# The first microseconds of a graph layer: first pieces shared between two DMA queues, four parts for piece 0, 17 warm-ups, and a_lo in halves to piece 19

## The chip, the cores and the metric

The kernel runs on one core of a Trainium2 chip. A core has TensorE (matrix multiply), VectorE and ScalarE (elementwise work), GpSimd, SyncE (which here only issues transfers), and 16 DMA engines that move data between HBM and the on-chip memory SBUF. Engines run on their own and wait for each other through semaphores. The metric is the time of one execution on the device in microseconds, the median of several runs.

## The reference: what is computed

```python
def _layernorm(x, axis=-1, eps=1e-05):
    m = jnp.mean(x, axis=axis, keepdims=True)
    v = jnp.var(x, axis=axis, keepdims=True)
    return (x - m) / jnp.sqrt(v + eps)

def reference(x, adj, L0_gnn_h):          # x: 8192x128, adj: 8192x8192, L0_gnn_h: 8192x128, float32
    h = jnp.maximum(_layernorm(x, axis=-1), 0.0)
    return x + 0.9 * (adj @ h) + 0.1 * L0_gnn_h
```

(Condensed to its core.) The work is the product of a 256 MB matrix with a small one. Each element of `adj` is read once and used for one 128-wide row of h.

## The kernel before

The contraction runs over 64 blocks of 128 rows of x (`BLOCKS`). The output has 16 chunks of 512 rows (`CHUNKS`), each one PSUM bank wide. `adj` comes in 256 pieces of 1 MB, each 128 x 2048 floats: 128 rows of the contraction for four chunks, or four times 128 rows for one chunk. The first 128 pieces are "wide": for each block k, piece 2k covers chunks 0 to 3 and piece 2k+1 chunks 4 to 7, so all eight banks are filled side by side. The other 128 are "tall": 16 pieces in a row complete one of chunks 8 to 15. The host stores pieces 0 to 23 as two halves (`early_dram`), so that each half is a transfer of its own; the others are one transfer each.

The product is made in three passes of a faster 32-bit format, fp32r. ScalarE rounds a piece to `a_hi` (L284), VectorE makes the rest `a_lo` = raw - a_hi (L328), and h is split likewise into `h_hi` and `h_lo`. TensorE does, per piece, four matmuls a_hi x h_hi (L416), four a_hi x h_lo (L422) and four a_lo x h_hi (L427); for tall pieces the lines are L438, L439 and L443. Only pieces 0 and 1 (`NATIVE`) go unsplit, as plain fp32 matmuls of raw and `h_full` (L405), which need nothing but the transfer and block 0 of h; each such matmul appears in the trace as two passes.

The order on each engine is written by hand:

- SyncE (the `sync` block) issues x of block 0, then pieces in order. `raw` has 6 slots; pieces 6 and 7 wait until TensorE has used pieces 0 and 1, later ones until VectorE has made a_lo of the piece six before. x of later units of four blocks goes ahead of a certain piece by the table `LOAD_X_AT`, for unit 2 (blocks 8 to 11) ahead of piece 5.
- ScalarE issues x of blocks 1 to 3 and 4 to 7 (L273, L274), scales blocks 1 to 3 (L251), rounds them (L258), then rounds the pieces; `SCALE_AT` and `HIGH_H_AT` say behind which piece later units are scaled and rounded.
- VectorE makes statistics (L294, L304, L307) and normalises block 0 on its own (L355, L359), does units 0 and 1, makes `h_lo` of unit 0 (L320), then a_lo of the pieces. `STATS_AT`, `AGGREGATE_AT`, `SHIFT_AT` and `LOW_H_AT` say behind which piece the steps of later units come. GpSimd makes 1/sqrt(var) between `aggregate` and `make_shift`, and VectorE waits for it in `make_shift`.
- TensorE runs 15 matmuls on zeros (`WARM_UP`, L399), then the pieces. `a_hi` and `a_lo` have 3 slots.

`EARLY` = 24 pieces are loaded and rounded in halves, `EARLY_LOW` = 10: pieces 2 to 9 have a_lo made in halves, each with its own count of the semaphore that TensorE waits for.

## Time and profile before

| | us |
|---|---|
| median of 3 runs | 711.0 |
| lowest and highest | 710.96 and 711.1 |
| the profiled execution | 711.17 |
| its span, first to last instruction | 709.4 |
| TensorE busy in it | 703.6 (99%) |
| VectorE busy | 627.1 (88%) |
| ScalarE busy | 524.4 (74%) |
| DMA, mean over the span | 403 GB/s |

The span is shorter than the execution by 1.8 us of start and end. Times below are from the start of the span. In the trace PE is a matmul on TensorE, PEld its weight load (which overlaps), DVE is VectorE, ACT ScalarE, POOL GpSimd, and SPq and ACTq are the instructions by which SyncE and ScalarE issue a transfer. What stands in brackets behind a row is the idle time of the engine before it and what ended it. The end of a matmul is modelled, so spacings of starts are to be read, not durations.

### The profile page before, as it was taken

Reading aid. Unit: us, or ns where it says so; the run is one execution under the profiler, and the core shown is the slowest. Engines: PE = TensorE matmul, PEld = TensorE weight load, DVE = VectorE, ACT = ScalarE, POOL = GpSimd, SP = SyncE. Lnnn points to the kernel's source line nnn. Section 1 sums busy time; section 2 is a strip of 40 time slices with the busy share of each in tenths; the row PEclk is TensorE's granted clock in tenths of the full one; section 3 lists DMA queues with packets and bytes.
Section 4 is the critical chain, followed back from the end, with each engine's and each line's share of the span. In section 5 each row is a group of like instructions: output and inputs, shape, how many; then the busy total and the mean of one; then the engine's idle time right before and its main releaser. Section 6 shows DMA issues by size and latency. Waiting matters only on the chain.

```text
span 709.4 us, 7934 instructions
## 1 busy us (share of the span) xinstructions
PE 703.6 (99%) x3079; PEld 577.5 (81%) x3079; DVE 627.1 (88%) x474; ACT 524.4 (74%) x356; POOL 39.7 (6%) x23
## 2 busy tenths in 40 slices
PE   8999999999999999999999999999999999999998
PEld 4878888888888888888888888888888888888886
DVE  5889999999999989999898888888988898889885
ACT  5888787888777878788767677776767676767673
POOL 1001111011010111010000000000000000000000
PEclk9999999999999999999999999999999999999999
DMA  9999999999999999999999999999999999999990
GB/s 353 409 408 412 421 419 417 423 417 418 421 419 420 421 419 420 419 419 422 414 401 413 394 396 396 404 385 405 419 421 421 421 420 423 420 420 422 404 418 18
DMA packets 47557, 285.73 MB, mean 403 GB/s; under 512 B 5280, under 2 KB 5792, under 8 KB 17824
## 3 DMA queue, kind: packets, MB, share of 16 engines
q1 hardware_dynamic: 47232, 284.77, 98.2%
q8 instruction: 24, 0.39, 0.2%
q10 hardware_dynamic: 288, 0.46, 0.2%
q14 instruction: 13, 0.11, 0.0%
HBM read 281.02 MB, written 4.19 MB: 402 GB/s over the span
## 4 chain that ended last, share of the span: by engine, by line
PE 94%; DMA 3%; DVE 1%; SPq 1%; ACT 1%; issue 0%; DVEq 0%
PE acc L443 16%; PE acc L438 16%; PE acc L439 16%; PE acc L427 15%; PE acc L422 15%; PE acc L416 15%; DMA raw<-early_dram 3%; DVE a_lo L328 1%; SPq L206 1%; ACT a_hi L284 0%; ACT h_full L251 0%; DVE finished L347 0%; SPq L191 0%; DVEq L119 0%; DVEq L346 0%
## 5 line engine op out<-in xcount | busy, mean ns | idle before, releaser
L328 DVE TENSOR_TENSOR a_lo<-raw,a_hi 128x2048 fp32r<-128x2048 f32 (+1 forms) x262 | 581.4, 2225 | 59.4 <-ACT a_hi L284 58.6
L284 ACT ACTIVATE a_hi<-raw 128x2048 fp32r<-128x2048 f32 (+1 forms) x276 | 491.4, 1782 | 169.4 <-PE acc L443 100.1
L438 PE MATMUL acc<-a_hi,h_hi 128*128 128x512 f32 x512 | 199.2, 389 | 0.0
L439 PE MATMUL acc<-a_hi,h_lo 128*128 128x512 f32 x512 | 199.2, 389 | 0.0
L443 PE MATMUL acc<-a_lo,h_hi 128*128 128x512 f32 x512 | 136.8, 389 | 0.0
L427 PE MATMUL acc<-a_lo,h_hi 128*128 128x512 f32 x504 | 135.1, 390 | 0.2 <-DVE a_lo L328 0.2
L416 PE MATMUL acc<-a_hi,h_hi 128*128 128x512 f32 x504 | 135.2, 390 | 0.0
L422 PE MATMUL acc<-a_hi,h_lo 128*128 128x512 f32 x504 | 134.7, 389 | 0.0
L438 PEld LDWEIGHTS acc<-a_hi,h_hi 128*128 128x128 f32 x512 | 96.1, 188 | 20.0
L443 PEld LDWEIGHTS acc<-a_lo,h_hi 128*128 128x128 f32 x512 | 96.1, 188 | 20.0
L439 PEld LDWEIGHTS acc<-a_hi,h_lo 128*128 128x128 f32 x512 | 96.1, 188 | 19.9
L427 PEld LDWEIGHTS acc<-a_lo,h_hi 128*128 128x128 f32 x504 | 94.4, 188 | 20.6 <-DVE a_lo L328 1.1
L416 PEld LDWEIGHTS acc<-a_hi,h_hi 128*128 128x128 f32 x504 | 94.6, 188 | 20.2 <-issue 0.5
L422 PEld LDWEIGHTS acc<-a_hi,h_lo 128*128 128x128 f32 x504 | 94.6, 188 | 19.7
L244 POOL TENSOR_TENSOR rstd<-var_eps,exponent 128x4 f32<-128x4 f32 (+2 forms) x17 | 39.2, 2304 | 279.4 <-DVE var_eps L307 279.4
L251 ACT ACTIVATE h_full<-x_sb,shift,rstd 128x128 f32<-128x128 f32 x63 | 27.1, 479 | 4.5 <-DVE shift L313 4.5
L294 DVE BATCH_NORM_STATS2 stats<-x_sb 128x6 f32<-128x128 f32 x64 | 17.9, 286 | 3.3 <-DMA x_sb<-x_dram 3.3
L347 DVE SCALAR_TENSOR_TENSOR finished<-acc,residual 128x512 f32<-128x512 f32 (+1 forms) x17 | 11.0, 652 | 3.9 <-PE acc L443 3.9
L313 DVE SCALAR_TENSOR_TENSOR shift<-mean_var,rstd 128x4 f32<-128x4 f32 (+1 forms) x16 | 2.6, 161 | 12.0 <-POOL rstd L244 12.0
L336 DVE SCALAR_TENSOR_TENSOR residual<-res_sb 128x512 f32<-128x512 f32 x16 | 10.9, 683 | 0.0
L320 DVE TENSOR_TENSOR h_lo<-h_full,h_hi 128x512 fp32r<-128x512 f32 x16 | 10.8, 676 | 0.0
L258 ACT ACTIVATE h_hi<-h_full 128x512 fp32r<-128x512 f32 x16 | 9.8, 614 | 0.1
(15 smaller groups left out, 29.4 us busy)
## 6 DMA issues: line engine op xcount, KB each, us to landing
raw<-tall_dram SPq DMA_DIRECT2D x128, 1024.0 KB, 8.0
raw<-wide_dram SPq DMA_DIRECT2D x104, 1024.0 KB, 11.1
raw<-early_dram SPq DMA_DIRECT2D x48, 512.0 KB, 11.7
res_sb<-res_dram SPq DMA_DIRECT2D x16, 512.0 KB, 9.8
out_dram<-finished SPq DMA_DIRECT2D x15, 256.0 KB, 8.2
x_sb<-x_dram SPq DMA_DIRECT2D x14, 256.0 KB, 11.5
x_sb<-x_dram ACTq DMA_DIRECT2D x1, 256.0 KB, 4.6
out_dram<-finished SPq DMA_DIRECT2D x2, 128.0 KB, 1.8
```

The costliest lines, as they stand in the source:

```text
L244: nc.gpsimd.tensor_tensor(rstd[:, a:b], var_eps[:, a:b], exponent[:, 0:b - a], ALU.pow).then_inc(rstd_ready, 1)
L251: last = nc.scalar.activation(h_full[:, in_h(k), :], x_sb[:, in_x(k), :], ACT.Relu, bias=shift[:, k:k + 1], scale=rstd[:, k:k + 1])
L284: nc.scalar.activation(a_hi[:, q % SPLIT_SLOTS, cols], raw[:, q % RAW_SLOTS, cols], ACT.Copy).then_inc(hi_ready, 1)
L294: return nc.vector.bn_stats(stats[:, k, :], x_sb[:, in_x(k), :])
L328: nc.vector.tensor_tensor(a_lo[:, q % SPLIT_SLOTS, cols], raw[:, q % RAW_SLOTS, cols], a_hi[:, q % SPLIT_SLOTS, cols].bitcast(fp32), ALU.s ...
L347: nc.vector.scalar_tensor_tensor(out=finished[:, n % 2, cols], in0=acc[:, c % WIDE, cols], scalar=1.0 - ALPHA, in1=residual[:, n % RES_RIN ...
L416: nc.tensor.matmul(acc[:, quad * QUAD + j, :], h_hi[:, k, :], a_hi[:, slot, cols], start=False, stop=False)
L422: nc.tensor.matmul(acc[:, quad * QUAD + j, :], h_lo[:, k, :], a_hi[:, slot, cols], start=False, stop=False)
L427: last = nc.tensor.matmul(acc[:, quad * QUAD + j, :], h_hi[:, k, :], a_lo[:, slot, cols], start=False, stop=(k == BLOCKS - 1))
L438: nc.tensor.matmul(bank, h_hi[:, k, :], a_hi[:, slot, cols], start=(k == 0), stop=False)
L439: nc.tensor.matmul(bank, h_lo[:, k, :], a_hi[:, slot, cols], start=False, stop=False)
L443: last = nc.tensor.matmul(bank, h_hi[:, k, :], a_lo[:, slot, cols], start=False, stop=(k == BLOCKS - 1))
```

## The change

- `EARLY_LOW` goes from 10 to 20: a_lo of pieces 10 to 19 is made in halves too.
- Piece 0 is loaded in four parts of 512 columns. Parts 1 and 3 of it and the second half of piece 1 (`BY_SCALAR`) are issued by ScalarE, the others by SyncE. x of block 0 is loaded in two halves of 64 partitions, one by each. ScalarE issues x of blocks 4 to 7 last.
- x of blocks 8 to 11 goes ahead of piece 7 instead of 5, and its statistics, aggregates and shift move with it; its scaling stays.
- VectorE makes h_lo of unit 0 ahead of the statistics of blocks 4 to 7, and the shift of unit 1 behind a_lo of piece 2.
- In the wide pieces TensorE does hi and lo on the first two segments, then hi and lo on the last two, then a_lo on all four.
- 17 warm-ups for 15.

```diff
-EARLY, EARLY_LOW = 24, 10
+EARLY, EARLY_LOW = 24, 20
 PARTS = {_q: 2 for _q in range(EARLY)}
+PARTS[0] = 4
...
+BY_SCALAR = [(0, 1), (0, 3), (1, 1)]
...
-LOAD_X_AT = {}
-STATS_AT, AGGREGATE_AT, SHIFT_AT = {}, {}, {}
...
+LOAD_X_AT = {7: 2}
+STATS_AT, AGGREGATE_AT, SHIFT_AT = {7: [8, 9], 8: [10, 11]}, {8: 3}, {NATIVE: 2, 10: 3}
...
-WARM_UP = 15
+WARM_UP = 17
...
+        def load_part(engine, q, i, cols):
+            n = PARTS[q]
+            at = (i % (n // 2)) * (PIECE // n)
+            engine.dma_start(raw[:, q % RAW_SLOTS, cols],
+                             adj_early[q, i // (n // 2), :, at:at + PIECE // n]
+                             ).then_inc(part_landed[q % RAW_SLOTS][i], 16)
...
+                if q in PARTS:
+                    for i, cols in parts(q):
+                        if (q, i) not in BY_SCALAR:
+                            load_part(sp, q, i, cols)
...
-            load_x(0, 0, 1)
+            sp.dma_start(x_sb[0:P // 2, 0, :], x[0:P // 2, 0, :]).then_inc(x_landed[0], 16)
...
+            act.dma_start(x_sb[P // 2:P, 0, :], x[P // 2:P, 0, :]).then_inc(x_landed[0], 16)
             act.dma_start(x_sb[:, 1:UNIT, :], x[:, 1:UNIT, :]).then_inc(x_landed[1], 16)
+            for q, i in BY_SCALAR:
+                load_part(act, q, i, dict(parts(q))[i])
             act.dma_start(x_sb[:, UNIT:2 * UNIT, :], x[:, UNIT:2 * UNIT, :]).then_inc(x_landed[2], 16)
...
+            low_h(0)
             for k in range(UNIT, 2 * UNIT):
                 wait_x(k)
                 last = statistics(k)
             last.then_inc(stats_ready, 1)
             aggregate(2)
-            make_shift(2)
-            low_h(0)
...
-                for j in range(QUAD):
...
+                for half in (range(0, QUAD // 2), range(QUAD // 2, QUAD)):
+                    for j in half:
...
+                        nc.tensor.matmul(acc[:, quad * QUAD + j, :], h_hi[:, k, :], a_hi[:, slot, cols],
+                                         start=False, stop=False)
...
+                    for j in half:
+                        cols = slice(j * SEG, (j + 1) * SEG)
+                        nc.tensor.matmul(acc[:, quad * QUAD + j, :], h_lo[:, k, :], a_hi[:, slot, cols],
+                                         start=False, stop=False)
```

VectorE at its start, before: from the statistics of blocks 1 to 3 to the a_lo of pieces 2 to 5 (`128x1024` is a half piece).

```order
L294 BN_STATS stats<-x_sb 128x6 x3
L304 BN_AGGR mean_var<-stats 128x2 x3
L307 TENSOR_SCALAR var_eps<-mean_var 128x3
L313 SCALAR_TENSOR_TENSOR shift<-mean_var,rstd 128x3
L294 BN_STATS stats<-x_sb 128x6 x4
L304 BN_AGGR mean_var<-stats 128x2 x4
L307 TENSOR_SCALAR var_eps<-mean_var 128x4
L313 SCALAR_TENSOR_TENSOR shift<-mean_var,rstd 128x4
L320 TENSOR_TENSOR h_lo<-h_full,h_hi 128x512
L328 TENSOR_TENSOR a_lo<-raw,a_hi 128x1024 x8
```

The same place in the changed kernel (its line numbers are 12 or 13 higher).

```order
L306 BN_STATS stats<-x_sb 128x6 x3
L316 BN_AGGR mean_var<-stats 128x2 x3
L319 TENSOR_SCALAR var_eps<-mean_var 128x3
L325 SCALAR_TENSOR_TENSOR shift<-mean_var,rstd 128x3
L332 TENSOR_TENSOR h_lo<-h_full,h_hi 128x512
L306 BN_STATS stats<-x_sb 128x6 x4
L316 BN_AGGR mean_var<-stats 128x2 x4
L319 TENSOR_SCALAR var_eps<-mean_var 128x4
L340 TENSOR_TENSOR a_lo<-raw,a_hi 128x1024 x2
L325 SCALAR_TENSOR_TENSOR shift<-mean_var,rstd 128x4
L340 TENSOR_TENSOR a_lo<-raw,a_hi 128x1024 x8
```

h_lo stands ahead of the second group of statistics, and the second shift has a_lo of piece 2 ahead of it.

ScalarE's start, before: two transfers of x, then its own work.

```order
L273 DMA x_sb<-x_dram 128x384
L274 DMA x_sb<-x_dram 128x512
L251 ACT_TABLE_LOAD
L251 ACTIVATE h_full<-x_sb,shift,rstd 128x128 x3
L258 ACTIVATE h_hi<-h_full 128x512
L284 ACTIVATE a_hi<-raw 128x1024 x4
```

And in the changed kernel.

```order
L282 DMA x_sb<-x_dram 64x128
L283 DMA x_sb<-x_dram 128x384
L184 DMA raw<-early_dram 128x512 x2
L184 DMA raw<-early_dram 128x1024
L286 DMA x_sb<-x_dram 128x512
L259 ACT_TABLE_LOAD
L259 ACTIVATE h_full<-x_sb,shift,rstd 128x128 x3
```

x of blocks 4 to 7 (`128x512`) is now the sixth transfer of this queue instead of the second.

## Rows read from the trace of the kernel before

**Rows 1.** The page, part 4: the chain that ended last, by engine.
```profile
PE 94%; DMA 3%; DVE 1%; SPq 1%; ACT 1%; issue 0%; DVEq 0%
```
**Rows 2.** Windows: stretch, us, busy us (count) of PE, PEld, DVE, ACT, POOL; PEclk; DMA.
```profile
100.00:200.00 100.00, 100.00 (x443) 82.81 (x442) 93.32 (x89) 80.89 (x62) 13.36 (x5) 1.00 1.02 420
600.00:700.00 100.00, 100.00 (x443) 82.81 (x442) 87.44 (x43) 71.00 (x37) 0.00 (x0) 1.00 0.93 383
```
**Rows 3.** Timeline of the start: start us, us, engine, line, operation, count.
```profile
1.10 3.38 PE L399 MATMUL acc<-warm 128*128 128x256 bf16 x15 [1.10 <-POOL warm L239]
...
4.79 0.29 DVE L359 TENSOR_SCALAR h_full<-x_sb,rstd 128x128 f32<-128x128 f32 x1 [0.63 <-POOL rstd L244]
...
5.71 8.66 PE L405 MATMUL acc<-raw,h_full 128*128 128x512 f32 x16 [1.23 <-DMA raw<-early_dram]
...
7.55 0.34 PEld L405 LDWEIGHTS acc<-raw,h_full 128*128 128x128 f32 x1 [0.52 <-issue]
...
8.40 0.34 PEld L405 LDWEIGHTS acc<-raw,h_full 128*128 128x128 f32 x1 [0.52 <-issue]
...
9.05 5.31 PE L405 MATMUL acc<-raw,h_full 128*128 128x512 f32 x12
```
**Rows 4.** Timeline of TensorE at pieces 3, 10 and 20.
```profile
16.98 1.07 PE L416 MATMUL acc<-a_hi,h_hi 128*128 128x512 f32 x4
...
38.17 1.20 PE L427 MATMUL acc<-a_lo,h_hi 128*128 128x512 f32 x4 [0.18 <-DVE a_lo L328]
...
64.03 1.08 PE L416 MATMUL acc<-a_hi,h_hi 128*128 128x512 f32 x4
```
**Rows 5.** Timeline of ScalarE: rounding the last half of piece 8 and piece 9.
```profile
28.17 1.06 ACT L284 ACTIVATE a_hi<-raw 128x1024 fp32r<-128x1024 f32 x1 [0.22 <-DMA raw<-early_dram]
30.89 1.06 ACT L284 ACTIVATE a_hi<-raw 128x1024 fp32r<-128x1024 f32 x1 [1.66 <-DMA raw<-early_dram]
32.17 1.06 ACT L284 ACTIVATE a_hi<-raw 128x1024 fp32r<-128x1024 f32 x1 [0.22 <-DMA raw<-early_dram]
```
**Rows 6.** DMA from 26.5 to 29 us: queue, packets, MB, share of 16 engines.
```profile
q8 instruction: 1, 0.02, 2.7%
```
**Rows 7.** Timeline: a_lo of piece 10, then pieces 25 to 27.
```profile
35.82 2.29 DVE L328 TENSOR_TENSOR a_lo<-raw,a_hi 128x2048 fp32r<-128x2048 f32 x1 [0.84 <-ACT a_hi L284]
...
74.28 1.92 ACT L284 ACTIVATE a_hi<-raw 128x2048 fp32r<-128x2048 f32 x1 [0.56 <-DMA raw<-wide_dram]
...
76.23 2.29 DVE L328 TENSOR_TENSOR a_lo<-raw,a_hi 128x2048 fp32r<-128x2048 f32 x1
...
82.20 2.29 DVE L328 TENSOR_TENSOR a_lo<-raw,a_hi 128x2048 fp32r<-128x2048 f32 x1
...
84.90 1.07 PE L427 MATMUL acc<-a_lo,h_hi 128*128 128x512 f32 x4
```
**Rows 8.** DMA issues before 1.5 us: count, KB, us from issue to landing.
```profile
raw<-early_dram SPq DMA_DIRECT2D x1, 512.0 KB, 4.4
x_sb<-x_dram ACTq DMA_DIRECT2D x1, 256.0 KB, 4.6
...
x_sb<-x_dram SPq DMA_DIRECT2D x1, 64.0 KB, 2.5
```
**Rows 9.** Timeline of VectorE: statistics of blocks 4 to 7, first a_lo.
```profile
7.28 0.87 DVE L294 BATCH_NORM_STATS2 stats<-x_sb 128x6 f32<-128x128 f32 x4
...
8.59 0.17 DVE L307 TENSOR_SCALAR var_eps<-mean_var 128x4 f32<-128x4 f32 x1
...
11.94 1.23 DVE L328 TENSOR_TENSOR a_lo<-raw,a_hi 128x1024 fp32r<-128x1024 f32 x1 [1.29 <-ACT a_hi L284]
```
**Rows 10.** Windows, as rows 2: the last two numbers are DMA share and GB/s.
```profile
4.00:4.50 0.50, 0.48 (x3) 0.00 (x0) 0.16 (x1) 0.00 (x0) 0.38 (x1) 1.00 0.97 356
...
5.00:5.50 0.50, 0.00 (x0) 0.00 (x0) 0.50 (x4) 0.00 (x0) 0.00 (x0) 1.00 1.04 410
5.50:8.00 2.50, 2.29 (x3) 1.18 (x4) 1.46 (x10) 0.60 (x2) 0.86 (x1) 1.00 1.03 419
```

34 lines of the change are left out of this document (11 added, 23 removed).

## The prediction, made before the changed kernel ran

> **What bounds the kernel now.** I read the chain of waits first, then the windows, the start of the timeline, the places where TensorE stalls, and last the transfers.
>
> The chain is TensorE for 94% of the span and DMA for 3% [rows 1]. Once it runs, TensorE is always busy: 443 matmuls in 100 us, in the wide half as in the tall half [rows 2]. From the hi-pass of piece 28 to the last matmul the spacing is 0.2267 us, and 12 × 0.2267 = 2.72 us make a piece. The change takes no matmul away, so all it can win is time in which TensorE was slow, idle or waiting. There are two such places.
>
> The start: warm-ups run to 4.48 us, the first real matmul starts at 5.71 with 1.23 us idle ahead of it, ended by a transfer; h_full was there at 4.79 + 0.29 = 5.08. Weight loads of the fp32 passes then start 0.85 us apart (7.55, 8.40); the twelve passes seen from 9.05 on start (5.31 − 0.59) / 11 = 0.43 apart [rows 3] (0.59 is one pass's own shown length). That is half speed and full speed, 1.2 and 2.4 GHz, though the granted clock reads 1.00 from 5.5 us on [rows 10].
>
> Early stalls: from the hi-pass of piece 3 (16.98) to that of piece 20 (64.03) it takes 47.05 us [rows 4], where 17 pieces need 17 × 2.72 = 46.24. So 0.81 us are lost, most of it ahead of piece 10's L427 at 38.17, where TensorE waits for a_lo [rows 4].
>
> What makes these stalls is the supply. A half piece lands every 1.28 us (30.89 and 32.17, where ScalarE starts on it), so a piece takes 2.56 us against TensorE's 2.72: the lead grows by 0.16 us a piece. And one landing came 1.44 us late (28.17 to 30.89 instead of 1.28) [rows 5]. In that stretch a single packet of queue 8, an instruction load, took 2.7% of 16 engines over 2.5 us, 1.07 us of one DMA engine [rows 6]. A half piece is spread over all engines and counts as landed with the last, so that one engine holds back every later landing.
>
> **The bound that the change doesn't touch.** After piece 20 TensorE never stalls, but its margins are thin, and the thinnest counts. It is piece 27's. ScalarE starts on piece 25 when it lands, at 74.28; VectorE makes a_lo of 25 from 76.23, then aggregates, a_lo of 26, a shift that waits for GpSimd, and a_lo of 27 from 82.20 to 84.49. TensorE begins on it at 84.90 [rows 7]. Where TensorE did stall, it started 0.06 us after a_lo: 35.82 + 2.29 = 38.11 [rows 7], then 38.17 [rows 4]. So the margin is 84.90 − 84.49 − 0.05 = 0.36 us. Pieces 24 to 27 keep whole loads and whole a_lo in the change, in the same VectorE order; their chain hangs on landings. **TensorE can arrive at piece 27 at most 0.36 us earlier; whatever more is won ahead of it becomes a wait there.**
>
> **Part by part.**
> x of block 0 in halves on two queues: whole, it took 2.5 us to land [rows 8]. Halved: 0 to 0.4 us earlier; I take 0.3, so h_full at 4.8.
> Piece 0 in four parts: its first half lands 4.4 us after issue now, together with x of 4 to 7 after 4.6 [rows 8], though that is 512 KB in 4 KB rows and this 256 KB in 2 KB rows: the two queues are served row by row. A first part of half the size, with x of 1 to 3 beside it alone, should land at 4.1 to 4.6, ahead of h_full.
> 17 warm-ups: fifteen filled 3.38 us [rows 3], two more at about 0.21 end near 4.9, where h_full comes. TensorE starts 0.8 us earlier, without a gap. The clock rises somewhere between the warm-ups' end and 8.7 as now: worth 0 to 1.6 us (three spacings of 0.85 and one of 0.66 against 0.43).
> Part (0,3) and half (1,1) wait their turn in their queues, to near 7.6 and 10.2, each about when TensorE wants them: 0 to 0.3 us lost. The fp32 pieces then end near 12 to 13 instead of 14.2.
> x of 4 to 7 is now the sixth transfer of ScalarE's queue and lands near 11 to 12 instead of 5.75. VectorE stands at it with its statistics, aggregates and var_eps, 7.28 to 8.76 now, 1.5 us [rows 9]; queued behind is a_lo of piece 2, which starts at 11.94 now [rows 9]. It will start at 12.3 to 13.6, and its two halves, 1.23 each with 1.14 between starts, end at 14.7 to 16.0; TensorE finishes the piece 0.45 later. So piece 3 starts at 16.0 to 16.8 (bounded below by the end of the fp32 pieces), say 16.4, against 16.98 now. Of some 2 us won at the start 0.6 is left here. ScalarE's scaling of blocks 4 to 7 waits some 0.4 us for the shift that stands behind this; the hi-pass has over 2 us of margin in pieces 4 to 6, which covers it.
> h_lo of unit 0 ahead of these statistics costs nothing; behind them it would have waited for x. The pass order hi, lo, hi, lo: the same matmuls, each with its own weight load before too; it wants the second half of a_hi 0.45 us later. A bank is revisited after two matmuls instead of four; tall pieces use one bank for all and run at 443 in 100 us too [rows 2].
> a_lo in halves to piece 19: two of 1.23 [rows 9] with overlapping starts, 2.37 us for 2.29 a piece, on an engine with idle time there. The first half comes 1.1 us earlier, and the last is wanted 0.45 later. The stalls up to piece 19 go: 0.81 us.
> x of 8 to 11 two pieces later: the halves of 5 and 6 land 0.64 us earlier, from 7 on nothing moves; its statistics move with it.
> The stream: same bytes, same engines, always some 10 us of transfers queued, so landings from piece 7 on move only if its rate does. While two queues were active it made 356 and later 410 GB/s, alone 419 [rows 10]. If two queues cost as in the first of these over 8 us, all lands 1.0 us later; if the start fills better, 0.3 earlier. I take 0.1 later, near the second.
> The Trainium skill ("Trainium Kernel Development and Optimization", Key Constraints) says that transfers of SP's and ACT's queues run on the same 16 engines, and that issuing from several only saves issue time. It speaks against any gain in the stream: by it the shift is 0 and the time 710.6.
>
> **The sum.** At piece 20 TensorE would be 0.6 + 0.81 = 1.4 us ahead; piece 27 lets 0.36 through; less 0.1 for the stream: 0.26. The profiled execution took 711.17 us with a span of 709.4; it would take 710.9 with 709.1. Against the median of 711.0: 710.7.
>
> **Rivals.**
> A, the forecast: capped at piece 27. With the stream's bounds of −0.3 and +1.0 the time is 710.3 to 711.6. Chance 0.70.
> B: the cap lifts. If the engine that was late at 30.89 isn't late before piece 25 (its load falls elsewhere), landings come up to 1.44 us earlier and the 1.4 us reach the end: 709.6, with a good start 709.4. For it: the load's time hangs on how far TensorE is in its program, which moves. Against: some engine always gets it. Chance 0.10.
> C, slower: two instruction loads fall on the same DMA engine. One did 1.44 us of harm, the later ones none that adds to it. If the next, near 58 us, adds, landings from piece 21 on come 1.44 later: 711.0 − 0.36 + 1.44 = 712.1, with 0.4 for two queues 712.5. It is a loss as soon as a_hi of piece 25 starts later than 74.28 + 0.36. Chance 0.10.
> D: x of 4 to 7 comes so late that VectorE holds TensorE up for good, or TensorE starts no earlier. Harmless until piece 3 starts after 16.98 + 0.81 − 0.36 = 17.4; beyond, each us costs one: 711.0 to 711.4. Chance 0.10.
>
> **How the numbers follow.** 0.2% is 1.4 us, about what a measurement can tell: below 709.6 is faster, above 712.4 slower. A and D lie within. Most of B is below (0.08), over half of C above (0.06); within: 0.86. A and D span 710.3 to 711.6; I widen to 709.9 and 711.7, which takes in what is near in B and C.
>
> **What would show it.** First real matmul near 4.9 without a gap behind the warm-ups; piece 3 between 16.0 and 16.8; no wait at pieces 10 to 19; new waits of TensorE for a_lo at pieces 20 to 27, some 1 us in all, the last at 27 with its a_lo ending near 84.5; a_hi of piece 25 starting within 0.3 us of 74.28. It would be wrong if piece 27's a_lo pass began more than 0.6 us ahead of 84.90, or if landings moved.

## The result and the profile after

| | before | after |
|---|---|---|
| median of 12 runs, us | 711.06 | 712.61 |
| lowest and highest | 710.96 and 712.06 | 712.25 and 713.21 |
| the profiled execution | 711.17 | 712.3 |
| its span | 709.4 | 710.5 |

The changed kernel is slower by 0.2%: after to before is 1.002, with a 95% interval of 1.0013 to 1.0028. The forecast of 710.7 and its range, to 711.7, missed. The spans of the two profiled executions, worked out to hundredths, are 709.35 and 710.47, so 1.12 us are to be explained. The medians lie 1.55 apart: the profiled execution of the changed kernel is one of its shorter ones, and the last experiment shows what a longer one looks like. Of all executions reported here four took 1018 to 4088 us; they move no median by more than 0.02 us, and of the two that were profiled (1845 and 1018 us) only the start is read.

The chain of waits of the changed kernel, by engine:

```profile
PE 97%; DMA 1%; DVE 1%; ACTq 0%; issue 0%; DVEq 0%
```

Read alone, this is better than the chain in [rows 1]: TensorE has 97% of it instead of 94. A share does not say how late TensorE was when it began to be busy. That stands in the timeline of the start (start us, us, engine, line, operation, count, idle before and what ended it):

```profile
0.74 0.57 SPq L225 DMA_DIRECT2D x_sb<-x_dram  x1
0.75 0.57 ACTq L282 DMA_DIRECT2D x_sb<-x_dram  x1
...
1.35 0.85 ACTq L283 DMA_DIRECT2D x_sb<-x_dram  x1
...
3.75 0.29 DVE L306 BATCH_NORM_STATS2 stats<-x_sb 128x6 f32<-128x128 f32 x1 [3.75 <-DMA x_sb<-x_dram]
...
5.28 0.29 DVE L372 TENSOR_SCALAR h_full<-x_sb,rstd 128x128 f32<-128x128 f32 x1 [0.63 <-POOL rstd L252]
```

x of block 0 is there at 3.73, not 0.3 us earlier than its 3.24 before but 0.5 later, and h_full starts at 5.28 against 4.79 in [rows 3]. The first real matmul gains almost nothing: 5.62 against 5.71. Then the timeline of TensorE to piece 3:

```profile
5.62 2.07 PE L417 MATMUL acc<-raw,h_full 128*128 128x512 f32 x2 [0.71 <-DVE h_full L372]
8.05 6.89 PE L417 MATMUL acc<-raw,h_full 128*128 128x512 f32 x14 [0.36 <-DMA raw<-early_dram]
14.38 1.02 PE L430 MATMUL acc<-a_hi,h_hi 128*128 128x512 f32 x2
...
17.20 0.73 PE L441 MATMUL acc<-a_lo,h_hi 128*128 128x512 f32 x2 [0.42 <-DVE a_lo L340]
18.34 0.73 PE L441 MATMUL acc<-a_lo,h_hi 128*128 128x512 f32 x2 [0.40 <-DVE a_lo L340]
18.91 0.63 PE L430 MATMUL acc<-a_hi,h_hi 128*128 128x512 f32 x2
```

TensorE waits for the second part of piece 0 until 8.05, and in piece 2 twice for a_lo. Four spacings of that piece are too long by 0.585, 0.114, 0.567 and 0.110, 1.38 us in all. Piece 3 starts at 18.91 instead of 16.98 in [rows 4]: 1.93 us late, of which 0.58 are there when piece 2 starts (14.38 against 13.80 before). VectorE shows why, at the place of [rows 9]:

```profile
14.54 0.87 DVE L306 BATCH_NORM_STATS2 stats<-x_sb 128x6 f32<-128x128 f32 x4 [3.51 <-DMA x_sb<-x_dram]
15.44 0.38 DVE L316 BATCH_NORM_AGGREGATE mean_var<-stats 128x2 f32<-128x6 f32 x4
15.85 0.17 DVE L319 TENSOR_SCALAR var_eps<-mean_var 128x4 f32<-128x4 f32 x1
15.93 2.35 DVE L340 TENSOR_TENSOR a_lo<-raw,a_hi 128x1024 fp32r<-128x1024 f32 x2
```

It stood for 3.51 us at x of blocks 4 to 7, which landed at 14.51 (5.75 before), with a_lo of piece 2 queued behind. After piece 3 TensorE never waits for an operand again; the 0.81 us lost between pieces 3 and 20 before (the waits at 10, 13 and 19) are gone. 1.93 − 0.81 = 1.12 us is the whole difference of the spans.

A second limit lies just beside it. ScalarE, VectorE and TensorE at pieces 25 to 27, as in [rows 7]:

```profile
75.62 1.92 ACT L296 ACTIVATE a_hi<-raw 128x2048 fp32r<-128x2048 f32 x1 [0.56 <-DMA raw<-wide_dram]
...
83.46 0.16 DVE L325 SCALAR_TENSOR_TENSOR shift<-mean_var,rstd 128x4 f32<-128x4 f32 x1 [0.90 <-POOL rstd L252]
83.54 4.49 DVE L340 TENSOR_TENSOR a_lo<-raw,a_hi 128x2048 fp32r<-128x2048 f32 x2
...
86.03 1.08 PE L441 MATMUL acc<-a_lo,h_hi 128*128 128x512 f32 x4
```

Piece 25 comes at 75.62 instead of 74.28: the stream of pieces is 1.34 us late there. a_lo of piece 27 starts at 83.54, takes 2.29 and ends at 85.83, 0.20 before TensorE wants it, so the margin is 0.15. Had TensorE not been late by itself, this would have made the kernel −0.36 + 1.34 = 0.98 us slower.

Where the stream lost its time stands in the windows, as [rows 10] (the last two numbers are DMA share and GB/s). The changed kernel:

```profile
3.50:4.00 0.50, 0.50 (x4) 0.36 (x3) 0.24 (x1) 0.00 (x0) 0.00 (x0) 1.00 0.80 166
4.00:4.50 0.50, 0.50 (x5) 0.29 (x2) 0.43 (x4) 0.00 (x0) 0.00 (x0) 1.00 0.87 219
4.50:5.00 0.50, 0.41 (x2) 0.00 (x0) 0.15 (x1) 0.39 (x1) 0.40 (x1) 1.00 0.91 229
5.00:5.50 0.50, 0.00 (x0) 0.00 (x0) 0.22 (x1) 0.50 (x1) 0.16 (x1) 1.00 0.93 264
6.00:7.00 1.00, 1.00 (x2) 0.12 (x1) 0.93 (x7) 0.00 (x0) 0.00 (x0) 1.00 1.07 424
...
2.00:9.00 7.00, 5.93 (x17) 2.69 (x16) 2.43 (x13) 1.97 (x3) 1.42 (x2) 1.00 0.91 302
```

and the kernel before, over the last of these stretches:

```profile
2.00:9.00 7.00, 5.77 (x16) 2.96 (x15) 3.68 (x22) 2.45 (x5) 1.58 (x3) 1.00 1.00 378
```

From 4 to 5.5 us the change moved 219 to 264 GB/s where [rows 10] has 356 to 410. From 6 us on both run at full rate, with two queues active too (424). Over 2 to 9 us it is 302 against 378, (378 − 302) × 7 us = 0.53 MB, which at 410 GB/s is 1.3 us. The loss is made before 6 us.

The trace holds sixteen completions for each transfer, one of each DMA engine, and the transfer counts as landed with the last. For the second half of piece 7 the mean of the sixteen is 1.41 us later than before and the last one 1.59; for piece 25 it is 1.40 and 1.34. So the mean loss stays as it was made. What changes on the way is the last engine, and the table of the stream below comes back to it.

### The profile page after: what moved, and what is told of

It reads as the page before. It is cut to its first block, busy times and chain, and to the rows that moved or that the text cites. A ratio compares the mean times of both kernels' runs of the same rounds, so it can differ in the third digit from the quotient of the medians.

```text
span 710.5 us, 7951 instructions
## 1 busy us (share of the span) xinstructions
PE 704.3 (99%) x3081; PEld 577.6 (81%) x3081; DVE 626.6 (88%) x484; ACT 523.6 (74%) x356; POOL 40.4 (6%) x23
## 3 DMA queue, kind: packets, MB, share of 16 engines
q10 hardware_dynamic: 800, 1.54, 0.6%
## 4 chain that ended last, share of the span: by engine, by line
PE 97%; DMA 1%; DVE 1%; ACTq 0%; issue 0%; DVEq 0%
PE acc L457 16%; PE acc L453 16%; PE acc L452 16%; PE acc L441 16%; PE acc L436 16%; PE acc L430 16%; DMA x_sb<-x_dram 1%; DVE a_lo L340 0%; ACTq L184 0%; DVE stats L306 0%; ACTq L283 0%; ACTq L282 0%; DVE finished L359 0%; DVE mean_var L316 0%; DVEq L122 0%
## 5 line engine op out<-in xcount | busy, mean ns | idle before, releaser
L452 PE MATMUL acc<-a_hi,h_hi 128*128 128x512 f32 x512 | 199.2, 389 | 0.0
L453 PE MATMUL acc<-a_hi,h_lo 128*128 128x512 f32 x512 | 199.2, 389 | 0.0
L430 PE MATMUL acc<-a_hi,h_hi 128*128 128x512 f32 x504 | 155.5, 390 | 0.0
L436 PE MATMUL acc<-a_hi,h_lo 128*128 128x512 f32 x504 | 155.2, 389 | 0.0
L306 DVE BATCH_NORM_STATS2 stats<-x_sb 128x6 f32<-128x128 f32 x64 | 17.7, 286 | 7.6 <-DMA x_sb<-x_dram 7.6
L417 PE MATMUL acc<-raw,h_full 128*128 128x512 f32 x16 | 9.0, 708 | 1.1 <-DVE h_full L372 0.7
## 6 DMA issues: line engine op xcount, KB each, us to landing
raw<-wide_dram SPq DMA_DIRECT2D x104, 1024.0 KB, 11.2
```

Source lines behind the costliest of these rows:

```text
L306: return nc.vector.bn_stats(stats[:, k, :], x_sb[:, in_x(k), :])
L430: nc.tensor.matmul(acc[:, quad * QUAD + j, :], h_hi[:, k, :], a_hi[:, slot, cols], start=False, stop=False)
L436: nc.tensor.matmul(acc[:, quad * QUAD + j, :], h_lo[:, k, :], a_hi[:, slot, cols], start=False, stop=False)
L452: nc.tensor.matmul(bank, h_hi[:, k, :], a_hi[:, slot, cols], start=(k == 0), stop=False)
L453: nc.tensor.matmul(bank, h_lo[:, k, :], a_hi[:, slot, cols], start=False, stop=False)
```

## The experiments

The questions: which part of the change makes the stream late; whether piece 27 is the cap that the forecast took it for; and whether late x of blocks 4 to 7 alone sets the time. The expectations name three theories of the late stream: S1, small rows in the first microseconds (the four parts of piece 0); S2, two queues with many transfers side by side; S3, the halves of x of block 0. Kernels from the changed side come first. Ratios are to the kernel before in the same batch, whose medians were 711.0 to 711.1. "Piece 25" is where ScalarE starts on it (before: 74.28), "piece 3" where TensorE does (16.98). Readings are of one profiled execution each. The diffs show the lines that matter; VectorE's count for x of block 0 (16 when it is whole, 32 in two halves) goes with each.

**The computation of the change with the transfers of before.**

```diff
-PARTS[0] = 4
...
-BY_SCALAR = [(0, 1), (0, 3), (1, 1)]
+BY_SCALAR = []
...
-            sp.dma_start(x_sb[0:P // 2, 0, :], x[0:P // 2, 0, :]).then_inc(x_landed[0], 16)
+            sp.dma_start(x_sb[:, 0, :], x[:, 0, :]).then_inc(x_landed[0], 16)
...
-            act.dma_start(x_sb[P // 2:P, 0, :], x[P // 2:P, 0, :]).then_inc(x_landed[0], 16)
```

> The changed kernel with the transfers of the start put back (x of block 0 whole, both halves of pieces 0 and 1 issued by SyncE, x of 4 to 7 second on ScalarE's queue); x of 8 to 11 ahead of piece 7, 17 warm-ups, the pass order and a_lo in halves to piece 19 stay. Theory 1 (all of the loss comes from the start's transfers, and what is won is capped at piece 27): 710.7 us, 0.36 below the kernel before; a_hi of piece 25 starts at 74.3 as before, a_lo of piece 27 ends near 84.5 and TensorE waits for it; no wait at pieces 10 to 19. Rival (the pass order, the halves of a_lo or the moved statistics cost something themselves): 711.4 us or more, with waits of TensorE in pieces 2 to 20 or a matmul spacing over 0.2267 us.

Median 710.96 (710.75 to 711.3), ratio 0.9998 [0.9988, 1.0007]; profiled 710.75, its shortest, with a span of 708.95, 0.40 less than before. By the medians the gain is 0.15 and inside the interval. Piece 25 at 74.13, no wait at pieces 10 to 19. VectorE and TensorE at piece 27:

```profile
82.05 4.49 DVE L338 TENSOR_TENSOR a_lo<-raw,a_hi 128x2048 fp32r<-128x2048 f32 x2
...
84.44 1.15 PE L439 MATMUL acc<-a_lo,h_hi 128*128 128x512 f32 x4
```

82.05 + 2.29 = 84.34, and TensorE goes on at 84.44, 0.10 later, in the one too long spacing (by 0.07) after piece 2. It is 0.46 us earlier than the 84.90 of [rows 7] and is just touched by the cap. In this profile the cap stands. The 1.65 us between this median and the changed kernel's come from the transfers put back here.

**All transfers on SyncE, still halves and quarters.**

```diff
-BY_SCALAR = [(0, 1), (0, 3), (1, 1)]
+BY_SCALAR = []
```

> The changed kernel with the three transfers of pieces 0 and 1 that ScalarE issued given back to SyncE; piece 0 stays in four parts of 2 KB rows, x of block 0 in halves. Landings from piece 7 on came 1.35 us later in the changed kernel (a_hi of piece 25 at 75.6 instead of 74.3). Theory S2 (the delay comes from two queues with many transfers issued at once): a_hi of piece 25 at 74.3 to 74.6, time 710.7 to 711.0. Theory S1 (it comes from small rows while the DMA engines start): at 75.2 or later, time 711.7 to 712.0. In both, x of 4 to 7 lands before 8 us and piece 3 starts before 16.5.

Median 712.11, ratio 1.0013 [1.0004, 1.0023]. x of 4 to 7 came early (7.37) and piece 3 started at 16.48. But TensorE waited at pieces 8 and 9 (1.54 us in all), and again at 21, 24 and 27, for piece 25 came only at 75.57. The stream is 1.29 us late with one queue for the pieces. S2 has lost its main case.

**Piece 0 in two halves, the second halves of 0 and 1 on ScalarE.**

```diff
-PARTS[0] = 4
-BY_SCALAR = [(0, 1), (0, 3), (1, 1)]
+BY_SCALAR = [(0, 1), (1, 1)]
```

> The changed kernel with piece 0 in two halves of 4 KB rows, one on each queue, like piece 1. Theory S1 (small rows cost the 1.35 us): a_hi of piece 25 back at 74.3 to 74.7; x of 4 to 7 still lands late, after 12.5, so piece 3 starts at 17 to 18 and the time is 711.0 to 711.6. Theory S2 (two queues cost it): a_hi of piece 25 at 75.4 or later, time 712.2 or more.

Median 711.8, ratio 1.001 [1.0001, 1.0019]. Piece 25 at 75.37, piece 3 at 18.65. At piece 25 two transfers fewer seem to give back only 0.25 us. But the halves of pieces 9 to 18 landed 0.6 us later than before instead of 1.34, and 0.5 was added near 60 us, by a cause that the table of the stream shows. So the quarters were more than half of the loss.

**x of 4 to 7 ahead of ScalarE's parts.**

```diff
+            act.dma_start(x_sb[:, UNIT:2 * UNIT, :], x[:, UNIT:2 * UNIT, :]).then_inc(x_landed[2], 16)
             for q, i in BY_SCALAR:
                 load_part(act, q, i, dict(parts(q))[i])
-            act.dma_start(x_sb[:, UNIT:2 * UNIT, :], x[:, UNIT:2 * UNIT, :]).then_inc(x_landed[2], 16)
```

> The changed kernel with x of blocks 4 to 7 ahead of the three transfers of pieces 0 and 1 on ScalarE's queue. VectorE then has its statistics early, and piece 3 starts near 16.5 to 17.5 instead of 18.91. If the late x alone decides the end: 711.2 to 711.5 (1.1 to 1.4 better than the change). If there are two limits side by side, the late x and the late stream (piece 27's chain, 0.15 us behind it): only 0.1 to 0.2 us better than the change, 712.1 to 712.5, and TensorE waits for a_lo at piece 27 instead.

Median of 4 runs 714.38, ratio 1.0049 [1.0034, 1.0064]: the slowest of all. It lies above both values expected, neither of which had the parts in mind. The edit moved the parts back as well, and part (0,1) landed at 10.39. TensorE, then its weight loads:

```profile
4.90 1.13 PE L417 MATMUL acc<-raw,h_full 128*128 128x512 f32 x2 [0.49 <-DVE h_full L372]
10.44 4.11 PE L417 MATMUL acc<-raw,h_full 128*128 128x512 f32 x5 [4.41 <-DMA raw<-early_dram]
```

```profile
12.20 0.34 PEld L417 LDWEIGHTS acc<-raw,h_full 128*128 128x128 f32 x1 [0.52 <-issue]
13.05 0.34 PEld L417 LDWEIGHTS acc<-raw,h_full 128*128 128x128 f32 x1 [0.52 <-issue]
...
14.39 0.19 PEld L417 LDWEIGHTS acc<-raw,h_full 128*128 128x128 f32 x1 [0.24 <-issue]
14.82 0.19 PEld L417 LDWEIGHTS acc<-raw,h_full 128*128 128x128 f32 x1 [0.24 <-issue]
```

After the wait the passes are 0.85 us apart until 13.9 and 0.43 after: 1.2 and 2.4 GHz, and the granted clock reads 0.50 from 11 to 14 us and 1.00 after. So this wait cost itself and slow passes behind it. Piece 3 started at 20.99.

**The change with x of block 0 whole.**

```diff
-            sp.dma_start(x_sb[0:P // 2, 0, :], x[0:P // 2, 0, :]).then_inc(x_landed[0], 16)
+            sp.dma_start(x_sb[:, 0, :], x[:, 0, :]).then_inc(x_landed[0], 16)
...
-            act.dma_start(x_sb[P // 2:P, 0, :], x[P // 2:P, 0, :]).then_inc(x_landed[0], 16)
```

> The changed kernel with x of block 0 as one transfer of SyncE again; four parts of piece 0 and the sharing of pieces 0 and 1 stay. Theory S3 (the halves of x of block 0 make the stream late: the three variants that had them started a_hi of piece 25 at 75.4 to 75.8, the one without at 74.1): a_hi of piece 25 at 74.1 to 74.6. x of 4 to 7 stays late, near 13.5, so piece 3 starts at 17.8 to 18.3 and the time is 711.3 to 711.8. Theory S1+S2 (rows and queues): a_hi of piece 25 at 75.2 or later and the time of the change, 712.2 to 712.6.

Median 711.92, ratio 1.0009 [0.9999, 1.002]: 0.7 us below the changed kernel's 712.61. x of 4 to 7 landed at 13.17 instead of 14.51 and piece 3 started at 17.59; piece 25 at 75.43, so waits at 24 and 27. S3 had asked for 74.1 to 74.6: the halves of x are not the whole cause.

Next the same parts, each added alone to the kernel before.

**Before, with x of block 0 in halves on two queues**, run twice, since the first profile serves for its start alone.

```diff
-            load_x(0, 0, 1)
+            sp.dma_start(x_sb[0:P // 2, 0, :], x[0:P // 2, 0, :]).then_inc(x_landed[0], 16)
...
+            act.dma_start(x_sb[P // 2:P, 0, :], x[P // 2:P, 0, :]).then_inc(x_landed[0], 16)
```

> The kernel before with x of block 0 in two halves of 64 partitions, one on each queue, and nothing else. Theory S3: a_hi of piece 25 at 75.3 or later, and since the kernel before had no margin in pieces 10 to 19, the time rises by all of it, to 712.1 to 712.4. Theory S1+S2: a_hi of piece 25 within 0.3 of 74.28, time 710.9 to 711.3.

> x of block 0 in partition halves on two queues, nothing else, a second time, since the profile of the first was taken while TensorE's clock stayed low and shows only the start. a_hi of piece 25 at 75.0 to 75.7, piece 10's wait for a_lo as in the kernel before but later, time 711.8 to 712.1.

Medians 711.96 and 711.68, ratios 1.0009 [0.9999, 1.0019] and 1.0009 [1.0, 1.0018]. Piece 25 at 74.73 in the second (+0.45): between what S3 (75.3 or later) and its rival (within 0.3 of 74.28) had asked for. Half of x takes as long as the whole:

```profile
x_sb<-x_dram SPq DMA_DIRECT2D x1, 32.0 KB, 2.1
x_sb<-x_dram ACTq DMA_DIRECT2D x1, 32.0 KB, 2.7
```

us from issue to landing of 32 KB each, where the whole 64 KB took 2.5 [rows 8]. VectorE needs both.

**Before, with piece 0 in four parts on SyncE.**

```diff
+PARTS[0] = 4
...
-        part_landed = [[sem(f"part_landed{s}_{i}") for i in range(2)] for s in range(RAW_SLOTS)]
+        part_landed = [[sem(f"part_landed{s}_{i}") for i in range(4 if s == 0 else 2)] for s in range(RAW_SLOTS)]
...
-                        source = adj_early[q, i, :, :]
+                        n = PARTS[q]
+                        at = (i % (n // 2)) * (PIECE // n)
+                        source = adj_early[q, i // (n // 2), :, at:at + PIECE // n]
```

> The kernel before with piece 0 in four parts of 2 KB rows, all issued by SyncE, x of block 0 whole. Theory S3: only the price of the rows, 0 to 0.3 us on the landings (a_hi of piece 25 at 74.3 to 74.6), time 711.0 to 711.4, TensorE's first real matmul near 5.2. Theory S1 (small rows in the slow phase): a_hi of piece 25 at 75 or later, time 711.9 or more.

Median 712.07, ratio 1.0013 [1.0004, 1.0023]. First real matmul at 5.45, piece 25 at 75.05 (+0.77), as S1 had said. The parts win 0.26 us at the start and lose 0.77 by piece 25.

**Before, with the second halves of pieces 0 and 1 on ScalarE**, the second queue alone.

```diff
+                    if (q, i) in ((0, 1), (1, 1)):
+                        continue
...
+            for q in (0, 1):
+                act.dma_start(raw[:, q, PART:PIECE], adj_early[q, 1, :, :]).then_inc(part_landed[q][1], 16)
             act.dma_start(x_sb[:, UNIT:2 * UNIT, :], x[:, UNIT:2 * UNIT, :]).then_inc(x_landed[2], 16)
```

> The kernel before with the second halves of pieces 0 and 1 issued by ScalarE ahead of x of 4 to 7; 4 KB rows, x of block 0 whole. This prices the second queue alone. So far, bytes moved by 9 us: 2.68 MB before, 2.35 with x in halves alone, 2.45 with four parts alone, 2.11 with all three. If the second queue costs little (what is left over in that table): 2.6 MB or more by 9 us, a_hi of piece 25 at 74.2 to 74.7, time 711.1 to 711.5. If it costs as the other two do: under 2.5 MB, a_hi of piece 25 at 74.9 or later, time 711.8 or more.

Median 711.18, ratio 1.0002 [0.9993, 1.0012]. Its profile is read at the start:

```profile
2.00:9.00 7.00, 5.22 (x16) 2.67 (x15) 2.34 (x13) 2.61 (x5) 1.42 (x2) 1.00 0.99 388
```

388 GB/s against 378, and piece 2 rounded from 10.85 on, as before. Sharing the pieces between two queues cost the stream nothing here, where their number and size stayed. It gains nothing either, as the rule cited in the prediction says (the Trainium skill, "Trainium Kernel Development and Optimization", Key Constraints).

**Before, with x of block 0 in halves, both on SyncE**: the opposite.

```diff
-            load_x(0, 0, 1)
+            sp.dma_start(x_sb[0:P // 2, 0, :], x[0:P // 2, 0, :]).then_inc(x_landed[0], 16)
+            sp.dma_start(x_sb[P // 2:P, 0, :], x[P // 2:P, 0, :]).then_inc(x_landed[0], 16)
```

> The kernel before with x of block 0 in two halves of 64 partitions, both issued by SyncE one behind the other. With one half on each queue, each issue took 0.57 us instead of 0.39, the next on ScalarE's queue 0.85, and the first data packet came at 2.10 us instead of 1.75. If the shape of 64 partitions makes that: issue again 0.55 or more, first packet near 2.1, a_hi of piece 25 at 74.9 or later, time 711.7 or more. If it is two queues issuing halves at once: first packet at 1.75, a_hi of piece 25 at 74.3 to 74.8 (piece 0 starts one issue later), time 711.0 to 711.5.

Median 712.87, ratio 1.0024 [1.0014, 1.0033], more than the whole change cost (1.002), from one additional transfer of 32 KB. Windows:

```profile
3.50:4.00 0.50, 0.50 (x4) 0.37 (x3) 0.00 (x0) 0.00 (x0) 0.00 (x0) 1.00 0.63 171
4.00:4.50 0.50, 0.48 (x3) 0.00 (x0) 0.00 (x0) 0.00 (x0) 0.00 (x0) 1.00 0.97 199
4.50:5.00 0.50, 0.00 (x0) 0.00 (x0) 0.22 (x1) 0.00 (x0) 0.00 (x0) 1.00 0.87 279
```

The hole of the changed kernel, on one queue. The first half of piece 0 was issued at 1.99 and took 5.0 us to land (4.4 in [rows 8]); piece 25 comes at 76.34. Of its 2.06 us 1.4 were added near 60 us, as the table of the stream shows: the halves of pieces 9 to 18 landed only 0.66 later than before.

**The same with halves by columns**, to see whether the 64-partition shape does it.

```diff
-            load_x(0, 0, 1)
+            sp.dma_start(x_sb[:, 0, 0:F // 2], x[:, 0, 0:F // 2]).then_inc(x_landed[0], 16)
+            sp.dma_start(x_sb[:, 0, F // 2:F], x[:, 0, F // 2:F]).then_inc(x_landed[0], 16)
```

> The kernel before with x of block 0 in two halves by columns: all 128 partitions, 64 columns (256 B rows) each, both issued by SyncE. With halves by partitions on one queue the issues took 0.56 us each, piece 0 was issued at 1.99 and its first half landed at 7.03, time 712.87. If the shape of 64 partitions is what costs: issues here near 0.39, piece 0's first half lands by 6.3, time 711.0 to 711.8. If two transfers ahead of piece 0 cost whatever their shape: lands near 7, time 712.3 to 713.

Median of 7 runs 713.55, ratio 1.0031 [1.002, 1.0041]. All 128 partitions, the same harm: first half of piece 0 landed at 8.00, piece 25 at 75.73. Here the start sets the time: the first real matmul is at 8.14, the passes are 0.85 us apart to 11.5, and piece 3 starts at 19.54, 2.56 late. What the two kernels have in common is the additional transfer ahead of piece 0. Each has a peculiarity of its own too (64 partitions there, rows of 256 B here), and neither peculiarity was tried without an additional transfer.

Then the other side, what the computation could win.

**The change with plain x, SyncE only, four parts, and a_lo in halves to piece 35.**

```diff
-EARLY, EARLY_LOW = 24, 20
+EARLY, EARLY_LOW = 24, 36
...
-BY_SCALAR = [(0, 1), (0, 3), (1, 1)]
+BY_SCALAR = []
...
-            sp.dma_start(x_sb[0:P // 2, 0, :], x[0:P // 2, 0, :]).then_inc(x_landed[0], 16)
+            sp.dma_start(x_sb[:, 0, :], x[:, 0, :]).then_inc(x_landed[0], 16)
...
-            act.dma_start(x_sb[P // 2:P, 0, :], x[P // 2:P, 0, :]).then_inc(x_landed[0], 16)
...
-                    dve.wait_ge(hi_ready, split_through(q, i if q in LOW_PARTS else None))
+                    dve.wait_ge(hi_ready, split_through(q, i if q in PARTS else None))
```

(Pieces 24 to 35 are still loaded and rounded whole, so both halves of their a_lo wait for the whole a_hi.)

> The changed kernel with x of block 0 whole, pieces 0 and 1 by SyncE alone (piece 0 in four parts), and a_lo in halves to piece 35 instead of 19. Theory of the cap: with piece 27's a_lo in halves its first half comes 1.1 us earlier and the last is wanted 0.45 later, so the wait at 27 goes and the margin there is some 0.8 instead of 0.36; TensorE is then bound by its own start (piece 3 at 16.5 to 17) and the time is 710.2 to 710.6, with no wait behind piece 3. Rival (halves past piece 19 change nothing, the landings decide): as with halves to 19, 710.9 to 711.0.

Median 711.04, ratio 0.9997 [0.9987, 1.0006], above the 710.2 to 710.6 expected: piece 3 started only at 17.39, and TensorE waited 0.3 us at piece 9. Piece 25 at 75.15 and no wait at 27. Halves lift the cap: with the stream 0.87 late, whole a_lo would have cost 0.5.

**The same with piece 0 in two halves**, that is, the transfers of before. Run twice, first and second "g2" below.

```diff
-PARTS[0] = 4
```

> The start's transfers as in the kernel before, a_lo in halves to piece 35, the rest as in the changed kernel. Theory of the cap: no wait at piece 27, the end follows TensorE's own start; piece 3 at 17.0 to 17.4 gives 0.45 to 0.8 us less than the kernel before, 710.3 to 710.7, below both kernels. Rival (nothing behind piece 19 mattered): the same as with halves to 19, 710.9 to 711.0.

> The best version (the start's transfers of before, a_lo in halves to piece 35) a second time in five rounds: 710.2 to 710.6, ratio to the kernel before 0.999, interval all below 1. In a profile with the stream as early as before (a_hi of piece 25 by 74.4) no wait of TensorE for a_lo behind piece 3 and a span of 708.6 to 708.9.

Medians 710.4 (10 runs, 710.18 to 711.13) and 710.26 (11 runs, 710.08 to 710.68), both ratios 0.999, the second's interval 0.9981 to 0.9999: **faster than both kernels**, by 0.7 us (0.1%) against before; the first one's interval, 0.9981 to 1.0, just reaches 1. In the second g2 profile, around piece 27, VectorE, then TensorE:

```profile
81.27 4.70 DVE L338 TENSOR_TENSOR a_lo<-raw,a_hi 128x1024 fp32r<-128x1024 f32 x4
```

```profile
83.93 1.07 PE L439 MATMUL acc<-a_lo,h_hi 128*128 128x512 f32 x4
```

0.97 us earlier than 84.90, past the cap of whole a_lo; the span is 1.0 shorter. VectorE's chain came earlier too: GpSimd's power took 1.92 us beside halves instead of 2.99. Part of this profile is luck. Its fp32 passes ran 0.43 us apart nearly from the first on and piece 3 started at 15.59, where the first g2 profile, of the same program, has 17.23. And it waited 1.09 us at pieces 8 and 9, against the expectation of no wait behind piece 3: with TensorE that early, the next limit is the landing that comes late near 29 us (ScalarE starts at 27.15 and 29.52 on halves that otherwise come 1.28 apart).

The first g2 profile was of one of its longer executions (711.09), with piece 25 at 75.11 though its transfers are those of before. ScalarE's rows near 60 us show where this came from:

```profile
58.20 1.06 ACT L294 ACTIVATE a_hi<-raw 128x1024 fp32r<-128x1024 f32 x1 [0.21 <-DMA raw<-early_dram]
60.49 1.06 ACT L294 ACTIVATE a_hi<-raw 128x1024 fp32r<-128x1024 f32 x1 [1.23 <-DMA raw<-early_dram]
```

The first of these halves is 0.2 us earlier than in the kernel before (58.42), the second 0.8 later (59.71), and so is all behind it. An instruction load (one packet of queue 8, 1.07 us long) starts at 57.35, as the one of [rows 6] does ahead of the late landing there.

**The change with the statistics of 4 to 7 moved behind a_lo of piece 2.**

```diff
-STATS_AT, AGGREGATE_AT, SHIFT_AT = {7: [8, 9], 8: [10, 11]}, {8: 3}, {NATIVE: 2, 10: 3}
+STATS_AT, AGGREGATE_AT, SHIFT_AT = {7: [8, 9], 8: [10, 11]}, {8: 3}, {3: 2, 10: 3}
...
-            for k in range(UNIT, 2 * UNIT):
-                wait_x(k)
-                last = statistics(k)
-            last.then_inc(stats_ready, 1)
-            aggregate(2)
...
                 low_a(q)
+                if q == NATIVE:
+                    for k in range(UNIT, 2 * UNIT):
+                        wait_x(k)
+                        last = statistics(k)
+                    last.then_inc(stats_ready, 1)
+                    aggregate(2)
```

(Scaling, rounding and h_lo of that unit go one piece later.)

> The changed kernel with VectorE's statistics of blocks 4 to 7 behind a_lo of piece 2, their shift behind piece 3, and scaling, h_hi and h_lo of that unit one piece later; the transfers stay as changed. This takes away the wait of a_lo for the late x. Piece 3 should start at 17.0 to 17.7 instead of 18.91, with no wait in piece 2. If the changed kernel has two limits side by side, the late stream holds: a_hi of piece 25 at 75.6 as there, TensorE waits 1.0 to 1.4 us for a_lo in pieces 20 to 27, time only 0.1 to 0.2 better, 712.2 to 712.5. If the late x was the whole loss: 711.2 or less.

Median 712.37, ratio 1.0017 [1.0007, 1.0026], only 0.24 below the change, which is less than the changed kernel's own medians differ (next experiment). The waits for a_lo in piece 2 are gone, yet TensorE waits at 24 and 27 (its weight loads):

```profile
77.62 0.77 PEld L442 LDWEIGHTS acc<-a_lo,h_hi 128*128 128x128 f32 x4 [0.36 <-DVE a_lo L340]
...
86.07 0.76 PEld L442 LDWEIGHTS acc<-a_lo,h_hi 128*128 128x128 f32 x4 [0.38 <-DVE a_lo L340]
```

Piece 3 began at 18.45, not the 17.0 to 17.7 that I expected, as TensorE began no pass between 5.58 and 7.89, for want of part (0,1), and then ran at 0.85 us a pass to 11.2.

**The changed kernel itself, once more.**

> The changed kernel again, to see which of its readings repeat: a_hi of piece 25 at 75.3 to 75.8, x of 4 to 7 landing at 14 to 15, piece 3 at 18.5 to 19.1, time 712.3 to 712.8.

Median of 4 runs 713.74, ratio 1.0035 [1.0021, 1.0048]. The expectation (712.3 to 712.8) missed, and the same kernel's medians in two batches, 712.61 and 713.74, differ by 1.1 us: a difference of some tenths between variants of the changed kernel says little by itself. The profiled execution (713.68) shows what a longer one consists of:

```profile
5.03 1.65 PE L417 MATMUL acc<-raw,h_full 128*128 128x512 f32 x2
8.96 5.40 PE L417 MATMUL acc<-raw,h_full 128*128 128x512 f32 x8 [2.29 <-DMA raw<-early_dram]
```

h_full was early this time and part (0,1) was not: a wait of 2.29 us, then passes 0.85 apart to 12.9, with the granted clock at 0.50 from 10 to 12 us. x of 4 to 7 landed at 15.78, piece 3 began at 20.20.

**All of them together.** The end moves by the larger of two shifts: TensorE's own, piece 3 minus 16.98 minus 0.81 for the stalls that no longer come; and the supply's, piece 25 minus 74.28 minus 0.36. All in us, from one profile each.

| whole a_lo from piece 20 | TensorE's | supply's | larger | span, measured |
|---|---|---|---|---|
| computation only | −0.45 | −0.51 | −0.45 | −0.40 |
| x of block 0 whole | −0.20 | +0.79 | +0.79 | +0.89 |
| halves, not quarters | +0.86 | +0.73 | +0.86 | +0.86 |
| the change | +1.12 | +0.98 | +1.12 | +1.12 |
| SyncE only | −1.31 | +0.93 | +0.93 | +1.22 |
| statistics later | +0.66 | +1.17 | +1.17 | +1.29 |
| the change again | +2.41 | +1.18 | +2.41 | +2.42 |
| x of 4 to 7 first | +3.20 | +1.15 | +3.20 | +3.17 |

One row is off by 0.3. Of that, 0.11 is the second spacing after the wait at 27, which is too long as well, and 0.15 lies behind the last matmul (3.75 us to the end instead of 3.61). In two rows the first column is too low, since TensorE waited again ahead of piece 20: with SyncE only 1.54 us at pieces 8 and 9, with x of block 0 whole 0.44 at piece 9. At piece 20 they stand at +0.31 and +0.33; the supply's shift is the larger one all the same.

The stream, by the rate over 2 to 9 us, and how much later than before its pieces came: for the second half of piece 7 the mean of the sixteen completions and the last of them, and piece 25.

| | GB/s | piece 7, mean, us | piece 7, last | piece 25 |
|---|---|---|---|---|
| second queue alone | 388 | −0.13 | +0.11 | not read |
| second g2 | 381 | −0.02 | +0.27 | −0.09 |
| before | 378 | 0 | 0 | 0 |
| computation only | 377 | +0.03 | +0.35 | −0.15 |
| first g2 | 369 | +0.11 | +0.78 | +0.83 |
| halves, not quarters | 349 | +0.60 | +1.03 | +1.09 |
| four parts | 346 | +0.50 | +0.91 | +0.77 |
| x halves, two queues (second run) | 339 | +0.71 | +0.95 | +0.45 |
| four parts, a_lo halves | 336 | +0.67 | +0.96 | +0.87 |
| x of block 0 whole | 329 | +0.86 | +1.23 | +1.15 |
| x halves, SyncE | 321 | +0.98 | +2.15 | +2.06 |
| x by columns, SyncE | 317 | +1.00 | +2.24 | +1.45 |
| SyncE only | 313 | +1.11 | +1.27 | +1.29 |
| the change, two profiles | 302, 290 | +1.41, +1.59 | +1.59, +2.71 | +1.34, +1.54 |
| statistics later | 301 | +1.43 | +1.51 | +1.53 |
| x of 4 to 7 first | 280 | +1.74 | +1.85 | +1.51 |

Every kernel with the transfers of before in number and size stands at 369 or above, every one with additional or smaller ones at 349 or below. The mean follows the rate nearly row by row. By the means, the four parts cost 0.50 us, the halves of x on two queues 0.71, the second queue alone nothing, and parts and halves together 1.11. The second queue beside four parts adds some 0.2 to 0.4 (1.41 against 1.11, 0.86 against 0.50 or 0.67), where two profiles with the same transfers differ by up to 0.18: so it is free by itself, and perhaps not in this company.

The landing counts with the last engine, and two things move that one. The start does, unevenly: with x halves on SyncE the mean loses 0.98 and the last engine 2.15. And the instruction loads do. There is one near 28 us in the kernel before and between 27 and 31 in the others. Before, it makes the last of the sixteen stand 1.47 us behind the next; with x halves on SyncE it shows in no landing, which is why these stand at +0.66 behind piece 9 and not at +2.15. A second one near 58 us adds nothing before and in the change. With x halves on SyncE it adds 1.4:

```profile
59.08 1.06 ACT L285 ACTIVATE a_hi<-raw 128x1024 fp32r<-128x1024 f32 x1 [0.20 <-DMA raw<-early_dram]
61.75 1.06 ACT L285 ACTIVATE a_hi<-raw 128x1024 fp32r<-128x1024 f32 x1 [1.61 <-DMA raw<-early_dram]
```

In the first g2 profile it adds 1.05 and with halves, not quarters, 0.5. In the kernel with x by columns 0.5 come already at 57.3 us, behind a smaller instruction load at 56.0. So the shift of piece 25 mixes what the start cost with how the loads fell. Which engine a packet ran on stands in no trace; that the load hit an engine that was late already is read from the completions, of which with x halves on SyncE the last stands 0.10 us behind the next ahead of it and 1.41 after it.

## Why the prediction was wrong, step by step

- **The term that failed is the stream, taken as 0.1 later with bounds of −0.3 and +1.0; it measured 1.34 at piece 25 and 1.59 at piece 7.** I priced a second queue, by rates of stretches in which two queues were active, and had no price for the additional and smaller transfers. The second queue alone is free (388 against 378, 424 at 6 us). What the change did to the first 6 us was a thing that no row of before showed, and my upper bound came from a row about something else (356 against 419 GB/s over 8 us, which is 1.2 us and not 1.0). The late start of the stream also brought down the terms of TensorE's own start: piece 3 was forecast at 16.4 and came at 18.91, and in the profile it is this that sets the end, with the stream's own limit 0.14 us behind. The reason against a change of rate ("same bytes, same engines, always some 10 us queued") holds only once the stream is at full rate.
- x of block 0, "0 to 0.4 us earlier": 0.5 later. Size does not set its landing (32 KB took 2.1 and 3.0 us, 64 KB 2.5), and both halves are waited for. The first issues took 0.57, 0.57 and 0.85 us, against 0.39, 0.41 and 0.46 before, and the first data packet moved at 2.10 us against 1.75. It is the halves by partitions that are slow to issue and not the two queues: on SyncE alone they took 0.56 and 0.58 as well, the halves by columns 0.38 and 0.42.
- Piece 0's first part, "4.1 to 4.6, ahead of h_full": 4.56. Right. But TensorE needed h_full, and that came 0.5 later, so the first matmul won 0.09 us instead of 0.8. Then part (0,1), landed at 8.01, stopped it. The prediction asked only for the first part and for (0,3) and (1,1); of (0,1) it says nothing.
- x of 4 to 7, "near 11 to 12": 14.51. The reasoning on what hangs behind it was right link by link: VectorE stands at it, a_lo of piece 2 behind, TensorE 1.38 us. Only the time was off by 2.5 to 3.5 us, from the same slow start and from its place in the queue (5.75 before, when it was second). This is rival D: "harmless until piece 3 starts after 17.4; beyond, each us costs one", counted from the 0.36 that the forecast wins. Piece 3 started at 18.91, 1.48 past the point, and −0.36 + 1.48 = 1.12 is what was measured. I gave D a price of 711.0 to 711.4, which lets it go past its point by 0.8 at most.
- Stalls at pieces 10 to 19, "go: 0.81 us": they went, here and in the kernel with the computation alone. The prediction didn't see that a TensorE that is early enough meets the same late landing sooner: in the four profiles in which the late landing came at the second half of piece 8 and piece 3 had started before 17.6, it waited at piece 8 or 9.
- The cap at piece 27, "at most 0.36 us earlier": borne out. With the old transfers the profile ends 0.40 earlier and touches it; halving a_lo there too lifts it, 710.26 against 710.96 in the medians.
- The pass order, h_lo ahead of the statistics and the later x of 8 to 11 at no cost: nothing in the trace of the computation-only kernel speaks against it. None of the three was run alone, nor were the 17 warm-ups: there the first real matmul came at 6.05 and piece 3 at 17.34, 0.36 later than before, as the first half of piece 0 landed 0.34 later in that profile.
- Rival C, a second instruction load that adds to the first, did not happen in the change. It did in two other profiles, with steps of 1.42 us (x halves on SyncE) and 1.05 (first g2), near the 58 us and the 1.44 that C names. C's mechanism is real, and that the change was spared it is luck. Rival B did not happen.
- The cited rule held: no gain in the stream from a second queue. It does not speak of a loss, and the loss came from the other half of the edit.

So the computation was forecast fairly: alone it has 710.75 in its profile against my 710.9, though by the medians it wins 0.15 us and not 0.3 (710.96 against 711.11). The edits of transfers turned that into a loss, by two ways of about the same size (1.12 and 0.98). Removing either one alone leaves the other, as "statistics later" and "SyncE only" show.

**What stays open.** Why an additional early transfer slows the first 6 us was not settled. An additional transfer ahead of piece 0 in its own queue costs more (means of 0.98 and 1.00, last engine 2.15 and 2.24) than halves on two queues (0.71 and 0.95), so the place in the queue matters as well as the number. Nor is it known which engine an instruction load takes, and so which execution gets one that adds.
